# Unread 128x256 products ahead of the work, normalising moved from GpSimd to ScalarE and VectorE, q by channel and turned in 32x32 blocks on VectorE, v as a plain product

## What is computed

```python
# block 0, one head
h = group_norm(x, 32 groups over pixels and 4 channels) * gn_scale + gn_bias
q, k, v = h @ wq + bq, h @ wk + bk, h @ wv + bv
scores = einsum('bqc,bkc->bqk', q, k) * C ** -0.5
x1 = einsum('bqk,bkc->bqc', softmax(scores), v) @ wo + bo + x
# block 1, linear attention, 8 heads of 16 channels
q, k, v = split(x1 @ w_qkv + b_qkv)
q = softmax(q, axis=channels of the head)
k = softmax(k, axis=tokens)
context = einsum('nelk,neld->nekd', k, v)
out = einsum('nekd,nelk->neld', context, q) @ w_out + b_out
y = x1 + out * sigmoid(gamma) + beta
```

## Time and profile before

| what | us |
|---|---|
| median of 3 runs (69.97 to 70.32) | 70.1 |
| the profiled execution | 70.25 |
| its span | 68.4 |
| busy: TensorE, its weight loads | 59.1, 54.1 |
| busy: GpSimd | 49.0 |
| busy: VectorE, ScalarE | 41.9, 41.6 |

### The profile page before, as it was taken

One profiled execution on the slowest core, in us unless ns is written; L12 is line 12 of the kernel. 1 busy time (PEld: TensorE's weight loads), 2 busy tenths in 40 slices (PEclk: granted clock), 3 DMA queues, 4 the chain that ended last, 5 costly groups with the idle time before them and its releaser, 6 DMA issues.

```text
span 68.4 us, 1147 instructions
## 1 busy us (share of the span) xinstructions
PE 59.1 (86%) x373; PEld 54.1 (79%) x373; DVE 41.9 (61%) x135; ACT 41.6 (61%) x133; POOL 49.0 (72%) x78
## 2 busy tenths in 40 slices
PE   2999999999968998897599999999999519899930
PEld 2898989879958787895599979999999317899810
DVE  2166957227998865489084868463878064984570
ACT  0722207417994998986299988778484093756600
POOL 4872910592899599999959899725999999873000
PEclk9999999999999999999999999999999995599999
DMA  0889500000000000000000000000000202002244
GB/s 0 227 193 327 214 0 0 0 0 0 0 10 5 0 5 0 0 0 5 0 0 0 0 10 0 0 0 0 0 0 0 77 0 77 0 10 77 77 156 150
DMA packets 2886, 2.77 MB, mean 40 GB/s; under 512 B 448, under 2 KB 2752, under 8 KB 2880
## 3 DMA queue, kind: packets, MB, share of 16 engines
q1 hardware_dynamic: 2448, 2.43, 11.5%
q10 hardware_dynamic: 432, 0.27, 1.3%
HBM read 1.64 MB, written 1.05 MB: 39 GB/s over the span
## 4 chain that ended last, share of the span: by engine, by line
PE 44%; POOL 33%; DVE 8%; DMA 6%; ACT 2%; issue 1%; SPq 1%
POOL probs L257 14%; POOL y_all L265 11%; PE bank L1054 6%; DMA xT_all<-in_x 6%; PE bank L1039 4%; PE bank L1048 4%; PE bank L1079 3%; PE bank L1033 3%; PE bank L1074 3%; PE bank L1084 3%; PE bank L1087 3%; POOL q L268 3%; PE bank L1029 3%; POOL hT_lo L252 2%; POOL x1T_lo L261 2%; DVE y_all L727 2%
## 5 line engine op out<-in xcount | busy, mean ns | idle before, releaser
L257 POOL TENSOR_SCALAR probs<-probs,s_inv 128x256 f32<-128x256 f32 x14 | 13.0, 945 | 1.9 <-DVE s_inv L694 1.8
L415 ACT ACTIVATE probs<-bank,neg_smax 128x256 f32<-128x256 f32 x16 | 7.5, 479 | 2.0 <-DVE neg_smax L691 2.0
L1054 PE MATMUL bank<-probsT,vals 128*128 128x256 f32 x32 | 8.1, 379 | 0.0
L1079 PE MATMUL bank<-k_exp,v 128*128 128x128 f32 x32 | 5.8, 320 | 2.3 <-ACT v L430 2.3
L691 DVE TENSOR_REDUCE neg_smax<-bank 128x2 f32<-128x512 f32 x8 | 5.5, 688 | 3.0 <-PE bank L1039 1.9
L265 POOL TENSOR_SCALAR y_all<-x1T,y_bias 128x256 f32<-128x256 f32 x8 | 7.3, 924 | 0.1
L1079 PEld LDWEIGHTS bank<-k_exp,v 128*128 128x128 f32 x32 | 5.3, 232 | 2.6 <-ACT v L430 2.5
L261 POOL TENSOR_TENSOR x1T_lo<-x1T,x1T_hi 128x256 fp32r<-128x256 f32 x8 | 5.8, 731 | 1.7 <-ACT x1T_hi L423 1.7
L1048 PE MATMUL bank<-ident,probs 128*128 128x128 f32 x32 | 5.0, 280 | 2.1 <-POOL probs L257 2.0
L420 ACT ACTIVATE probsT<-bank 128x512 f32<-128x512 f32 x8 | 4.8, 602 | 3.0 <-PE bank L1048 2.9
L433 ACT ACTIVATE q<-q 128x256 f32<-128x256 f32 x8 | 3.3, 428 | 4.9 <-POOL q L268 4.9
(11 more groups left out here) (116 smaller groups left out, 188.0 us busy)
## 6 DMA issues: line engine op xcount, KB each, us to landing
xT_all<-in_x SPq DMA_DIRECT2D x8, 128.0 KB, 3.9
out_y<-y_all SPq DMA_DIRECT2D x8, 128.0 KB, 1.7
one_s<-in_w_one SPq DMA_DIRECT2D x1, 320.0 KB, 4.1
qk_s<-in_w_qk ACTq DMA_DIRECT2D x1, 128.0 KB, 2.8
vo_s<-in_w_vo ACTq DMA_DIRECT2D x1, 128.0 KB, 4.1
vec<-in_vectors ACTq DMA_DIRECT2D x1, 5.0 KB, 3.0
```

Of the source, the lines that this page charges most:

```text
L257: p = pool.tensor_scalar(probs[:, b, j, :], probs[:, b, j, :], s_inv[:, b, j:j + 1], None, ALU.mult)
L415: e = act.activation(probs[:, b, j, :], full(S_PS[b])[:, j, :], ACT.Exp, bias=neg_smax[:, b, j:j + 1], accum_out=s_sum[:, b, j:j + 1])
L1054: m = pe.matmul(wide(ATT_PS[b]), vals[:, b, k, :], probsT[:, b, k, :], start=(k == 0), stop=(k == J - 1))
L1079: m = pe.matmul(square(CTX_PS[b]), v1[:, b, j, :], k_exp[:, b, j * C:(j + 1) * C], start=(j == 0), stop=(j == J - 1))
```

## The change

- **TensorE's start.** `gather_eps` and its tile go; the eps is added on VectorE by `add_eps` after the aggregation. The unread products are 11 at the head and 6 more after the first two gathers. Batch 1 comes first, then 0, 2 and so on.
- **Normalising of the probabilities.** Before: batch 0 on VectorE, seven on GpSimd with two `tensor_scalar` each. Now: 1, 3, 5 and 7 on ScalarE (two copies with a scale), 2 and 0 on VectorE, 4 and 6 on GpSimd as one `tensor_tensor` with the inverse sum stretched over the columns.
- **x1 plus bias** on GpSimd is a `tensor_tensor` with the bias stretched over the columns, and comes batch by batch as x1 is ready; the bias is made early.
- **q and v.** q is made channel by token (`qT_product`), copied with its bias as a column (`q_copy`, ScalarE), turned in 32x32 blocks (`q_blocks`, VectorE) so that the 16 channels of a head lie along the columns, and after the softmax turned back (`q_back`, VectorE). v is a plain product of its own (`v_product`). `q_bias`, `q_transposes` and `qT_copy` go.
- All five lists and the banks are written anew.

```diff
-        added_eps = sb("added_eps", [P, J, GC, J, 3])
+        q_c = sb("q_c", [P, B, L])
...
             def normal_probs(b):
-                for j in range(J):
-                    p = pool.tensor_scalar(probs[:, b, j, :], probs[:, b, j, :], s_inv[:, b, j:j + 1], None, ALU.mult)
-                p.then_inc(pn_pool, 1)
+                pool.tensor_tensor(probs[:, b, :, :], probs[:, b, :, :], s_inv[:, b, :].unsqueeze(2).to_broadcast([P, J, L]),
+                                   ALU.mult).then_inc(pn_pool, 1)
...
             def x1_plus_bias(b):
-                pool.tensor_scalar(y_all[:, b, :], x1T[:, b, :], y_bias[:, :], None, ALU.add).then_inc(x1b_ready, 1)
+                pool.tensor_tensor(y_all[:, b, :], x1T[:, b, :], y_bias[:, :].to_broadcast([P, L]), ALU.add).then_inc(x1b_ready, 1)
...
+            def normal_probs(b):
+                for j in range(J):
+                    p = act.activation(probs[:, b, j, :], probs[:, b, j, :], ACT.Copy, scale=s_inv[:, b, j:j + 1])
+                p.then_inc(pn_act, 1)
...
+            def q_copy(b):
+                act.activation(q_c[:, b, :], wide(QT_PS[b]), ACT.Identity, bias=vec[:, BQ1:BQ1 + 1]).then_inc(qc_ready, 1)
...
-            def qT_copy(b):
-                act.activation(qT[:, b, :], wide(QTR_PS[b]), ACT.Copy).then_inc(qT_ready, 1)
...
+            def add_eps(n):
+                a, z = STAT_SETS[n]
+                dve.tensor_scalar(mv[:, a:z, 1], mv[:, a:z, 1], EPS, None, ALU.add).then_inc(veps_ready, 1)
...
-            def q_bias(b):
-                dve.tensor_tensor(q[:, b, :].rearrange("p (j c) -> p j c", j=J), both(QV_PS[b])[:, :, 0, :],
-                                  bq1_b.unsqueeze(1).to_broadcast([P, J, C]), ALU.add).then_inc(qb_ready, 1)
...
+            def q_blocks(b):
+                dve.transpose(q[:, b, :], q_c[:, b, :]).then_inc(qblk_ready, 1)
+
+            def q_back(b):
+                dve.transpose(qT[:, b, :], q[:, b, :]).then_inc(qT_ready, 1)
...
-            def qv_product(b):
+            def qT_product(b):
+                split_product(wide(QT_PS[b]), w1_hi[:, 0, :], w1_lo[:, 0, :], x1T_hi[:, b, :], x1T_lo[:, b, :]).then_inc(qT_done, 1)
+
+            def v_product(b):
                 for j in range(J):
-                    rows = slice(j * P, (j + 1) * P)
-                    m = split_product(both(QV_PS[b])[:, j, :, :], x1T_hi[:, b, rows], x1T_lo[:, b, rows],
-                                      w1_hi[:, 0:3:2, :], w1_lo[:, 0:3:2, :])
-                m.then_inc(qv_done, 1)
+                    m = pe.matmul(pairs(V_PS[b])[:, j, :], x1T[:, b, j * P:(j + 1) * P], w1[:, 2, :], start=True, stop=True)
+                m.then_inc(v_done, 1)
...
-            turn_over(9)
-            pe.wait_ge(eps_ready, 1)
-            gather_eps(1)
+            turn_over(11)
...
+            turn_over(6)
```

More of the change, by code:

```diff
@@ L368, in _ @@
+            q_shift(0)
+            pool.wait_ge(qinv_ready, 4)
+            q_normal(3)
+            pool.wait_ge(x1T_ready, 8)
             x1_plus_bias(7)
@@ new lines, in _ @@
+            act.wait_ge(smax_ready, 7)
+            s_exp(6)
+            normal_probs(5)
+            x1T_high(3)
+            act.wait_ge(kmax_ready, 3)
+            k_exp_t(4)
+            act.wait_ge(qT_done, 3)
+            q_copy(4)
+            act.wait_ge(pT_done, 6)
+            pT_copy(5)
+            act.wait_ge(m_done, 1)
+            m_copy(1)
+            act.wait_ge(m_done, 2)
+            m_copy(2)
+            act.wait_ge(x1T_ready, 5)
+            x1T_high(0)
+            act.wait_ge(qT_done, 4)
@@ new lines, in _ @@
+            ctx_mask(1)
+            dve.wait_ge(q_ready, 2)
+            q_back(2)
+            dve.wait_ge(probs_ready, 7)
+            s_recip(6)
+            dve.wait_ge(kexp_ready, 3)
+            k_recip(4)
+            x1_sum(0)
+            dve.wait_ge(qc_ready, 3)
+            q_blocks(4)
+            dve.wait_ge(s_done, 8)
+            s_max(7)
+            dve.wait_ge(qblk_ready, 3)
+            q_maxima(4)
+            dve.wait_ge(y_done, 1)
+            y_sum(1)
+            dve.wait_ge(qc_ready, 4)
@@ new lines, in _ @@
+            x1_sum(6)
+            dve.wait_ge(q_ready, 3)
+            q_back(4)
+            dve.wait_ge(kT_done, 5)
+            k_max(0)
+            dve.wait_ge(qc_ready, 5)
+            q_blocks(0)
+            k_max(3)
+            dve.wait_ge(qblk_ready, 5)
+            q_maxima(0)
+            q_recip(3)
+            dve.wait_ge(kT_done, 6)
+            k_max(5)
+            dve.wait_ge(kexp_ready, 4)
+            k_recip(3)
+            dve.wait_ge(qc_ready, 6)
+            q_blocks(5)
@@ L1070, in k_transposes @@
                 t.then_inc(ktr_done, 1)
-            def q_transposes(b):
-                for j in range(J):
-                    t = pe.transpose(wide(QTR_PS[b])[:, j * P:(j + 1) * P], q[:, b, j * C:(j + 1) * C], ident[:, :])
-                t.then_inc(qtr_done, 1)
             def ctx_product(b):
@@ new lines, in _ @@
+            gather(4)
+            u_plain(0)
+            pe.wait_ge(spread_ready, 5)
+            gather(3)
+            pe.wait_ge(h_ready, 3)
+            val_product(2)
+            pe.wait_ge(one_in, 16)
+            y_bias_product()
+            pe.wait_ge(u_ready, 2)
+            s_product(0)
+            pe.wait_ge(h_lo_ready, 1)
+            u_product(2)
+            pe.wait_ge(h_ready, 4)
+            val_product(3)
+            val_product(0)
+            pe.wait_ge(pn_act, 1)
+            p_transposes(1)
@@ L1301 @@
     ins = {n: np.asarray(a) for n, a in inputs.items()}
-    columns = [ins[n].reshape(-1)[-C:] for n in VECTORS]
+    columns = [ins[n].reshape(-1)[-C:] for n in VECTORS] + [ins["L1_conv_b_qkv"][0:C]]
     q_row = np.broadcast_to(ins["L1_conv_b_qkv"][0:C], (C, C))
```

1180 lines of the change are left out of this document (568 added, 612 removed).

## The result

The changed kernel takes 62.28 us (median; 61.42 to 62.43) against 70.1 us before; the ratio is 0.884, 95% interval 0.872 to 0.896. Its profiled execution took 62.31 us with a span of 60.6 us; the span before was 68.4 us. Some executions of a kernel take longer than its others (of the kernel before 72 to 74 us, at a lower granted clock), and each ratio compares the shorter executions of both kernels. The time agrees with the forecast of 62.2 us. Two terms of the sum behind it do not, and they cancel.

The account below looks back on a forecast made before the run. The bound changes hands between TensorE and GpSimd. -1.5 - 2.4 - 1.0 - 4.3 + 1.2 = -8.0 takes the span from 68.4 to 60.4 us; plus 1.85 gives 62.2 us, range 59.3 to 66.5.

Parts of the forecast that it names:

- The start: TensorE's first products: batch 1 begins earlier and the clock may be up early; -1.5 us, taken as the middle.
- Both bounds: For TensorE's beginning: -2.8 us at most if the clock is up, +0.3 at worst if the six products delay the gather.
- 2 x 0.63 and 1.2: Savings in us on the two first plain products and on the score products if the clock is up early.
- the 0.3 ahead of it: Batch 1's first product starts near 8.7 us instead of 9.1, for -0.3 us.
- 18 to 36 us: TensorE's 2.5 us idle there, mostly waiting for GpSimd's normalising, nearly goes: -2.4 us, or -1.2 if new owners are late.
- 54 to 60 us: TensorE's 2.27 us wait, 0.35 behind it and 1.7 from half-rate products go: -4.3 us, or -2 if some remains.
- The hole and the half level: TensorE almost idle from 54 to 56.2 us, then its clock at 1.2 GHz from 56.2 to 59.9; both were to go.
- TensorE's work: New products for q and v, without q's transposes, save 1.2 us over eight batches; called -1.0 for smaller pieces' overhead.
- What is late next: New waits among TensorE, ScalarE and VectorE, with little room left on any: +1.2 us, bounds 0 and +5.
- The rival that the page stands beside: GpSimd is not relieved: two-operand additions cost twice the old form, GpSimd stays the bound from 48 us; 67.5 us, chance 0.03.
- a sign of trouble: ScalarE's normalising over 0.6 us each was named as one thing that would show the forecast wrong.
- ScalarE is late: ScalarE's four normalisations queue behind copies and exponentials, TensorE waits about 0.95 us each: +3.8, 66.0 us, chance 0.22.

Follow-up runs that it names:

- the twelve products: The changed kernel with 12 instead of 6 unread products behind the second gather: 58.28 us, ratio 0.830 to the kernel before.
- the form alone: The kernel before, with GpSimd's normalising as one two-operand product per batch and its bias additions in two-operand form: 64.61 us, ratio 0.921.

## Why the prediction was right, and where it was not

*The start: -1.5 forecast, +0.1 in the profiled execution.* This is the step that failed, "Whether the clock is up by then I cannot read ... I take -1.5, the middle". The middle between two outcomes was not an outcome. With six products the full level came at about 14 or 16.7 us, or came early and fell again; the forecast needed it early and lasting. Both bounds were also off: the twelve products, which do keep the level, bring the first transposes from 18.22 to 14.33 us, -3.9, where the lower bound was -2.8. What that bound counted behind the first plain product, 2 x 0.63 and 1.2, came as counted: from it to the transposes it is 6.6 us with the twelve and 9.1 before. What was too small is the 0.3 ahead of it: with the level up, the small products there are quicker too, and it begins at 7.72 instead of 9.10 us, 1.4 earlier. With six products it begins 0.8 earlier (8.31), and that was lost again: the level came at about 16.7 us, in the profile before at about 15.4.

*18 to 36 us: -2.4 forecast, -2.1 measured* (2.48 to 0.42 us idle). Right in size. Its reason was too narrow: it named the new owners of the normalising, and the form alone does the same with the old owner (0.35 us idle).

*54 to 60 us: -4.3 forecast.* The hole and the half level are gone, as said: outside of 18 to 36 us TensorE's idle time falls by 2.6 us (rows below), and the half level was 1.7. The early additions were given as the cause. The kernel with additions late and the one with short forms both show that the hole closes, or nearly, in either way, and that most of the time follows only when GpSimd's amount of work falls.

*TensorE's work: -1.0 forecast.* From the first transposes to the last product, TensorE was busy 41.50 us before and 38.21 after, -3.3; of this the half level was 1.7, which leaves -1.6. The stretch before, then after:

```profile
18.22:64.84 46.62, 41.50 (x297) 38.28 (x296) 30.58 (x95) 34.23 (x112) 38.87 (x52) 0.96 0.04 13
```

```profile
18.30:56.95 38.65, 38.21 (x290) 36.25 (x289) 34.23 (x103) 36.23 (x121) 25.24 (x38) 1.00 0.04 12
```

*What is late next: +1.2 forecast, about 0 measured.* In that stretch TensorE is idle for 0.44 us in all (38.65 - 38.21), 5.12 before. This mis-sized term hid the first: the start gave 1.6 us less, the tail 1.4 more (-7.9 against -2.4 - 1.0 - 4.3 + 1.2 = -6.5). That 62.28 lies so close to 62.2 is luck. The worry was sound even so: 2 us more on ScalarE or VectorE do make something late.

*Prices.* GpSimd 35.1 us (36 forecast), its normalising 1.04 (1.2), its additions 0.61 (0.62); VectorE 46.4 (46.5), its turns 0.43 and 0.42 (0.41); ScalarE 43.9 (46). The rule of the Trainium skill (GPSIMD Engine Reference, Engine selection), by which one-input operations run at roughly line rate on GpSimd and two-input ones about twice as slow as on VectorE, would make the old form the cheap one. These runs show the opposite: two one-input instructions of 0.945 us became one two-input instruction of 1.04 for the same elements. The rival that the page stands beside has fallen. On ScalarE the normalising takes 0.618 us, above the 0.6 that I had named as a sign of trouble, and there was none: these are durations of instructions that overlap (eight of 0.618 make 4.1 us busy), and in the chain of the kernel with more ScalarE work a pair moves on after 0.79 us.

*The rival "ScalarE is late"* (66.0 us, 0.22) did not come, but little was missing: eight more copies on ScalarE lengthen the tail by 3.5 us.

## What to carry to other kernels

When one engine's long pieces stand in the chain, first try a cheaper form of the same instruction, before moving work: here two edits of form gave 5.5 us, and moving the work in the queue without lessening it gave about 1.1. Work that only keeps TensorE's clock up paid here where it filled the pause behind which the level fell; with too little there it gave nothing back (61.5 us without any, 61.5 and 62.3 with 17 products). And a term that has two outcomes should be forecast as one of them, with the other as a rival: a mean of the two is right only by chance.

## What the runs showed of the hardware

The full level of TensorE's clock came at about 5.1, 14.0 and 16.7 us in kernels whose TensorE work up to 5 us is the same, the last two in two executions of one kernel; in two profiles a pause of 0.70 and 0.79 us between small products was followed by a fall. The clock row reads full from the start in the profiles whose level rises late, so that only the durations tell (1.19 against 0.68 us for the same four products). On GpSimd an instruction with a column operand by partition takes 0.92 to 0.95 us for 128x256 elements, and one with a second operand stretched over the columns 0.61 to 0.62; the subtractions of two whole tiles, whose result is stored as fp32r, take 0.73 to 0.79.
